# A graph network's decoder: the residual x is added by TensorE into PSUM, and VectorE takes its statistics from the banks

## What is computed

```
delta = relu(h @ Wd1 + bd1) @ Wd2 + bd2          # [1250, 256] -> 512 -> 1024
y     = layernorm(x + delta, out_g, out_b)       # gain and bias
out   = _layernorm(x + y)                        # no gain, no bias
```

## Time and profile before

| what | value |
|---|---|
| median of 3 runs | 642.91 us (642.67 to 643.5) |
| the profiled execution: its time | 642.69 us |
| the profiled execution: its span | 640.7 us |
| busy: PE, DVE, ACT, POOL | 90%, 66%, 31%, 17% of the span |
| granted TensorE clock, mean | 0.991 of full speed |
| the decoder's banks are written (line 863) | from 532.02 to 624.77 us |
| the output tiles on VectorE | from 553.38 to 633.9 us |

### The profile page before, as it was taken

How to read it: one execution, slowest core, us unless ns; L and a number is a source line. 1 busy time by engine, 2 the same in 40 slices (tenths; PEclk the granted TensorE clock), 3 DMA queues, 4 the chain that set the end, 5 groups by cost and what they waited for, 6 DMA issues and landing times.

```text
span 640.7 us, 8334 instructions
## 1 busy us (share of the span) xinstructions
PE 576.6 (90%) x2581; PEld 396.3 (62%) x2581; DVE 421.0 (66%) x1028; ACT 200.4 (31%) x417; POOL 107.6 (17%) x109
## 2 busy tenths in 40 slices
PE   0399999999998988988999999999999989989990
PEld 0355555555557665665588888886877855545440
DVE  6678888888885667767652122016758665899775
ACT  9123333333312345444242212112223222133221
POOL 9500000000000000000316443301202220132210
PEclk9999999999999999999999999999999999999996
DMA  8200000000002121011830000320000100012112
GB/s 244 70 33 33 33 32 32 32 32 32 33 3 83 33 58 39 33 59 46 205 128 25 0 0 1 102 105 1 10 25 0 33 1 0 1 57 71 54 53 86
DMA packets 20982, 30.71 MB, mean 48 GB/s; under 512 B 5537, under 2 KB 15243, under 8 KB 20952
## 3 DMA queue, kind: packets, MB, share of 16 engines
q1 hardware_dynamic: 20822, 30.07, 14.8%
q10 hardware_dynamic: 130, 0.26, 0.1%
HBM read 25.20 MB, written 5.12 MB: 47 GB/s over the span
## 4 chain that ended last, share of the span: by engine, by line
PE 77%; DVE 15%; ACT 4%; issue 2%; DMA 1%; POOL 1%; DVEq 0%; POOLq 0%; ACTq 0%
PE banks L644 18%; PE banks L781 11%; PE banks L703 10%; PE banks L863 8%; PE banks L617 5%; PE banks L673 5%; PE banks L793 4%; PE banks L803 4%; PE banks L713 3%; PE banks L853 2%; PE banks L677 2%; DMA xt<-in_x 1%; PE banks L625 1%; ACT x_first L439 1%; DVE x_first L1118 1%
## 5 line engine op out<-in xcount | busy, mean ns | idle before, releaser
L644 PE MATMUL banks<-w_all,xnT 128*125 128x429 f32 x320 | 130.0, 528 | 0.0
L863 PE MATMUL banks<-wd_s,dT 128*125 128x512 f32 x160 | 70.5, 595 | 1.8 <-DVE s L1256 1.0
L644 PEld LDWEIGHTS banks<-w_all,xnT 128*125 128x125 f32 x320 | 54.0, 189 | 28.9 <-issue 28.3
L703 PE MATMUL banks<-hT,w_s 128*128 128x250 f32 x320 | 69.0, 375 | 0.2
L703 PEld LDWEIGHTS banks<-hT,w_s 128*128 128x128 f32 x320 | 60.2, 189 | 9.2 <-issue 1.9
L617 PEld LDWEIGHTS banks<-oh_code,oh_low 125*128 125x128 bf16 x320 | 31.3, 98 | 45.6 <-issue 43.7
L728 PE MATMUL banks<-y_hi,adj 125*125 125x288 f32 x200 | 54.1, 300 | 2.1 <-DVE y_lo L1017 2.1
L617 PE MATMUL banks<-oh_code,oh_low 125*128 125x240 bf16 x320 | 48.0, 271 | 8.3 <-issue 8.3
L331 POOL TENSOR_SCALAR xh<-x_first,small 125x1024 f32<-125x1024 f32 x6 | 7.4, 1241 | 280.3 <-DVE adj L1104 280.1
L980 DVE TENSOR_TENSOR oh_code<-iota_c,edge 125x960 bf16<-125x960 f16 x82 | 53.4, 652 | 0.0
L730 PE MATMUL banks<-y_lo,adj 125*125 125x286 f32 x200 | 53.2, 294 | 0.0
(11 more groups left out here) (186 smaller groups left out, 902.6 us busy)
## 6 DMA issues: line engine op xcount, KB each, us to landing
xt<-in_x SPq DMA_DIRECT2D x20, 500.0 KB
out_x<-ot SPq DMA_DIRECT2D x9, 500.0 KB
w_s<-in_L_gnn_W SPq DMA_DIRECT2D x5, 512.0 KB, 10.6
w_all<-in_L_gnn_W_rel SPq DMA_DIRECT2D x2, 1144.0 KB, 11.2
wd_s<-in_L_gnn_Wd SPq DMA_DIRECT2D x1, 2048.0 KB, 13.7
w_all<-in_L_gnn_W_root SPq DMA_DIRECT2D x1, 1144.0 KB, 10.2
wo_s<-in_L_gnn_wo_weight SPq DMA_DIRECT2D x1, 1024.0 KB
wa_s<-in_L_gnn_layer_Wa SPq DMA_DIRECT2D x3, 256.0 KB, 2.8
```

The source lines that it names most:

```text
L644: ins = pe.matmul(pb[0:P, 2 + 2 * v + n, 0:FH], xnT[:, u], w_all[:, u, n * FH:(n + 1) * FH], start=(u == 0), stop=(u == KD - 1))
L703: ins = pe.matmul(pb[:, 4 + f % 2, 0:2 * P], w1_s[:, k, f * 128:(f + 1) * 128], hT[:, k], start=(k == 0), stop=(k == KD - 1))
L863: ins = pe.matmul(pb[0:P, 2 + 2 * u + q], dT[:, k, u * P:(u + 1) * P], wd2_s[:, k, q * 512:(q + 1) * 512], start=(k == 0), stop=(k == K1 - 1))
```

## The change

TensorE gets one more product at the head of each accumulation: the identity (`ident`, 125 x 125) as the stationary operand and 512 features of `x1` as the moving one. It opens the bank (`start=True`), and the four products with `wd2_s` add to it. After them the bank holds x + delta. VectorE's addition and its result in `s5` go; `bn_stats` reads the banks; the subtraction of the mean reads the banks too and writes `s5`. TensorE's wait for free banks is now for `o_gain`, which that subtraction raises, in place of `o_sum`. The wait for x (`xb_done`) moves from VectorE to TensorE, and VectorE's wait for ScalarE to have read `s5` (`f_done`) moves from the addition to the subtraction.

```diff
             def decode_2(c, u, q):
                 if q == 0:
                     pe.wait_ge(d1_done, 1 + c * K1 + K1)
+                    pe.wait_ge(xb_done, 2 * c + u + 1)
                     if c > 0:
-                        pe.wait_ge(o_sum, 2 * (c - 1) + u + 1)
+                        pe.wait_ge(o_gain, 2 * (c - 1) + u + 1)
+                pe.matmul(pb[0:P, 2 + 2 * u + q], ident[0:P, 0:P], x1(2 * c + u)[:, q * 512:(q + 1) * 512],
+                          start=True, stop=False)
                 for k in range(K1):
                     ins = pe.matmul(pb[0:P, 2 + 2 * u + q], dT[:, k, u * P:(u + 1) * P],
                                     wd2_s[:, k, q * 512:(q + 1) * 512],
-                                    start=(k == 0), stop=(k == K1 - 1))
+                                    start=False, stop=(k == K1 - 1))
@@ decoded(t)
                 dve.wait_ge(d2_mm, 1 + t + 1)
-                dve.wait_ge(xb_done, t + 1)
-                if t >= 2:
-                    dve.wait_ge(f_done, t - 1)
-                dve.tensor_tensor(s5[:, u], pb[0:P, 2 + 2 * u:4 + 2 * u].rearrange("p a b -> p (a b)"),
-                                  x1(t), ALU.add).then_inc(o_sum, 1)
-                dve.wait_ge(o_sum, t + 1)
-                dve.bn_stats(st5[:, u, 0], s5[:, u, 0:512])
-                dve.bn_stats(st5[:, u, 1], s5[:, u, 512:D]).then_inc(o_stats, 1)
+                dve.bn_stats(st5[:, u, 0], pb[0:P, 2 + 2 * u])
+                dve.bn_stats(st5[:, u, 1], pb[0:P, 3 + 2 * u]).then_inc(o_stats, 1)
@@ weighed(t)
                 dve.wait_ge(o_mv, t + 1)
-                dve.scalar_tensor_tensor(s5[:, u], s5[:, u], mv5[:, u, 0:1], go_b[:], ALU.subtract,
-                                         ALU.mult).then_inc(o_gain, 1)
+                if t >= 2:
+                    dve.wait_ge(f_done, t - 1)
+                dve.scalar_tensor_tensor(s5[:, u], pb[0:P, 2 + 2 * u:4 + 2 * u].rearrange("p a b -> p (a b)"),
+                                         mv5[:, u, 0:1], go_b[:], ALU.subtract, ALU.mult).then_inc(o_gain, 1)
```

## The result

The changed kernel takes 658.59 us (median of 4 runs, 657.7 to 659.01) against 642.79 us for the kernel before in the same comparison: a ratio of 1.0245, 95% interval 1.0229 to 1.026, slower by 15.8 us. The profiled execution took 659.01 us with a span of 657.0, which is 16.3 more than before's.

What follows compares the result with a forecast made beforehand. TensorE was taken to set the end from output chunk 2 on. The terms, 17.30 + 1.62 - 2.03 - 0.64 - 1.24 = +15.0 us on 642.69, with the median 0.2 higher, gave 657.9 us, range 656.4 to 660.4.

Steps and rivals of the forecast that it cites:

- 1. VectorE's first output tile: Chunk 0's four new products stand ahead of layer 3's last products, so VectorE's first output tile starts later: +3.46 us.
- 2. start of chunk 1: Before chunk 1, TensorE waits for `o_gain` of tile 0, raised later than the old addition's sign: +1.62 us.
- 3. length of chunk 1: Chunk 1 gets four identity products on TensorE: +3.46 us.
- 4. from chunk 1 to chunk 2: Between chunks 1 and 2, the wait caused by a late VectorE goes: -2.03 us.
- 5. chunks 2 to 4: Chunks 2, 3 and 4 get 12 identity products, with no gap on TensorE to cover them: +10.38 us.
- 6. tail: After TensorE's end, VectorE is ready for the last tile, -0.64 us, and has no addition, -1.24; the remaining 14.05 stays.
- The price: Each of 20 new float32 identity products with 512 moving columns costs TensorE 0.865 us, as line 863's products do.
- What was costed at nothing: VectorE's 1.24 us in nine of ten tiles, the `xb_done` wait and later bank release in chunks 2 to 4: 0.
- Reading the banks: VectorE's three operations reading PSUM instead of SBUF, on the path twice: taken as 0, bounds -0.4 and +1.1 us.
- A cheaper product: Rival: identity or back-to-back issue makes TensorE's product cost 0.44 or 0.25 us, giving 649.4 or 645.6 us; chance 0.06.
- Being held for the banks in each chunk: Rival: TensorE also waits for banks at chunks 2 to 4, 1.62 us each, 4.9 in all: 662.8 us; chance 0.04.
- VectorE as the bound: Rival: VectorE bounds the output chunks, so its shorter tiles save 12.4 us: 630.5 us; chance 0.03.

Runs made afterwards that it cites:

- undisturbed execution: The changed kernel run once more with nothing altered: its profiled execution, which had the same stop and no slow product, took 658.7 us; median 658.95 us.
- VectorE's part: The changed kernel without the identity product on TensorE, so x is missing from the first norm's input: 641.14 us against 642.77 for the kernel before.
- the rounded product with three pairs of banks: The changed kernel with identity and x + bd2 as rounded float32 and three pairs of banks in turn for output tiles: 642.16 us, ratio 0.9994 to before.
- the rounded product: The changed kernel with the identity and x + bd2 held as rounded float32, so the product takes one pass: 646.13 us against 642.76 for the kernel before.
- the last tile rounded: The kernel before with three pairs of banks, earlier relus of chunks 2 and 3, and a rounded identity product replacing the last tile's addition: 639.9 us, ratio 0.9953.

## Why the prediction was right

Each step of the sum against the traces, all from the first `turn_h` on:

| step | predicted | changed kernel, first profile |
|---|---|---|
| 1. VectorE's first output tile | +3.46 | 30.95 - 27.50 = +3.45 |
| 2. start of chunk 1, beyond step 1 | +1.62 | 33.95 - 28.86 - 3.45 = +1.64 |
| 3. length of chunk 1 | +3.46 | 18.95 - 13.90 = +5.05 |
| 4. from chunk 1 to chunk 2 | -2.03 | 4.15 - 6.17 = -2.02 |
| 5. chunks 2 to 4 | +10.38 | 60.30 - 49.96 = +10.34 |
| 6. tail: VectorE is ready | -0.64 | 0.04 - 0.64 = -0.60 |
| 6. tail: no addition | -1.24 | 7.54 - 8.77 = -1.23 |
| sum | +15.0 | +16.63 |

Step 3 is the one that was mis-sized, and only in that execution: at full clock chunk 1 is 17.26 us, +3.36. The undisturbed execution of the same kernel has +14.94 in sum. The two halves of the change measured alone fit it: +14.54 for the product and -2.32 for VectorE's part make 12.22, which is 2.7 less than 14.94; that is step 4's 2.03 and step 6's 0.64, a gain that either half makes by itself and both together make only once.

The table ends with the last issue. Step 6 also has what follows the addition keep its 14.05 us to the span's end. Up to the last issue it does. From there on are 6.52 us before and 7.30 and 7.45 in the two profiles of the changed kernel, 0.8 and 0.9 more, so that TensorE's end lies 14.87 us ahead of the span's end and not 14.1. Over the 14 profiles this piece varies by as much between kernels that end with the same program, and whether the change has a part in it stays open.

**The price** of 0.865 measured 0.858 when doubled. The form of the product, not the identity in it, sets the price: as rounded float32 the same operands cost 0.23. The Trainium skill's sustained rate for 512 columns (TensorE: Matmul & The Clock Gate, Back-to-back issue gap), taken four times as in the prediction, would have made it 0.52, an estimate; no row here agrees.

**What was costed at nothing** cost nothing. VectorE waits 1.9 us or more for the banks at every tile from the third on, 26.6 us in all. The release of the banks is never waited for after chunk 1's start. ScalarE's late square root did hold VectorE, 2.57 us at 581.98, and no one waited for VectorE there.

**Reading the banks** cost nothing within 5 ns an operation. The 62 cycles (0.065 us, an estimate) that the Trainium skill's cycle table adds for PSUM (VectorE: DVE Perf Modes, The TRN2 errata) are not there in these three forms. So the choice that the same page of the Trainium skill gives (Rules for kernel authors), to accept the 1x rate with PSUM as the source or to copy to SBUF first for many operations, had nothing to win by the copy here; no run tried it.

**A gap that was passed over.** The prediction says that TensorE never waits after 574.81 us and that chunks 2 to 4 ran without a gap. The earlier trace rows has one, 0.56 us for ScalarE's relu at 610.77, ahead of chunk 4. It changes nothing in the sum, since it stands at the same place with the same 0.56 us in the changed kernel.

**The rivals.** A cheaper product is refuted by the doubled one. Being held for the banks in each chunk is refuted by the timeline after, where chunks 2 and 3 start without a wait and chunk 4 has the 0.56 us for ScalarE that it had before. VectorE as the bound is refuted by its part alone, which gives 1.6 us and not 12.4, and by the rounded product with three pairs of banks, which gives nothing although VectorE's tiles are 12.4 us shorter in all and the products cost no more than 4.6.

**What I did not see**: that the wait of step 2 can cost more than its own length. The stop of 2.67 us was in the forecast, the clock was not. Of the five profiled executions with a stop of 2.65 to 2.67 us two show the half clock (the changed kernel's first, the rounded product), three don't (VectorE's part alone, the product twice, the changed kernel again), and the one with 4.08 us does. In the other eight profiles no stop of TensorE in the decoder reaches 2 us, and the granted clock is at full speed up to TensorE's last product. The medians, 15.8 and 16.3 us over before in two comparisons, are 0.8 and 1.3 over the sum. Two things lie there, a clock loss of 1.7 us in some of the executions and the 0.8 to 0.9 us behind the last issue, and the runs don't tell how much of the 0.8 and 1.3 each makes. No rival and no term of the range had either of them. The range held because it was 2.5 us wide above the forecast for other reasons (the banks, the price, two waits), and that part is luck. In which executions the clock falls is not settled by these runs.

## What to carry to other kernels

That a second engine is busy for nearly all of a stage (VectorE, 16.86 of 17.98 us) doesn't tell what a cheaper operation there would bring. Moving 1.2 us of a tile's work from an engine with slack to the one that bounds costs the whole new price, here 0.86 us for 512 columns, 1.7 for a tile. Here it paid only where the receiving operation is short (rounded, 0.23 us, which gives up digits of x) and the relieved engine is on the path: in the last tile, by 1.26 us of the decoder's stretch. When a counter's release moves behind more work, follow it to every place where it is waited for; the steady state may have 7 us of cover and the first turn none.

## What was not expected of the hardware

A stop of TensorE of 2.7 us cost the granted clock in two of five profiled executions. In the first profile it fell to 1.2 GHz about 0.6 us after work had begun again and stayed there from 559.3 to 562.7, in which the products took twice their time: 1.6 to 1.7 us lost, more than half of the stop once more. The moment differs: with the rounded product it fell 1.2 us after work had begun again, and in the stop of 4.08 us 0.3 us before.

The same is seen once in a stage that the change doesn't touch. All 14 profiles have a stop of 2.1 us at about 190 us, and in one of them, the last tile rounded, the clock was at half from 193.9 to 197.3. Three products whose results nobody reads, put into the stop ahead of chunk 1, made a decoder's stretch of 123.31 us: what the stop costs where the clock holds (123.24), and 1.62 less than where it fell.
